# A first transformer layer's out-projection as three rounded fp32r products instead of one fp32 product

## The chip, the cores and the metric

The kernel runs on one core of a Trainium2 chip. The metric is the device time of one execution in microseconds (us). A core has TensorE (PE; its weight loads are listed as PEld), VectorE (DVE), ScalarE (ACT), GpSimd (POOL) and a queue for DMAs on SyncE (SP). Each engine works through its own list of instructions in order and waits on semaphores for the others.

## What is computed

Two transformer layers over 64 x 188 tokens of width 256. Only the first one's attention and FFN touch the change:

```python
h = tok_ref(x, ...)                                  # strided conv, layer norm
h = h + attn_ref(layernorm(h), qkv_proj, qkv_bias, out_proj, out_bias)
h = h + ffn_ref(layernorm(h), w_gate, w_up, w_down)  # fp4-quantized
# in attn_ref: 16 heads of 16, softmax, then
out = einsum('lni,ei->lne', out, out_proj) + out_bias
```

The second layer (linear attention with a cumulative sum, and an FFN) is computed by another function, `layer1`, which the change leaves alone.

## The kernel before

`layer0` handles 94 tiles (`TILES`) of 128 tokens. Its work is a software pipeline: in slot t the conv of tile t, the attention of tile t-1, the out-projection of tile t-2, the FFN's gate and up products of tile t-3 and its down product of tile t-4 are done. `slots` writes out slots 0 to 5 and the last ones and loops over the rest, two slots a turn. Every engine has its own `slot` function, whose order of calls is the order of that engine's instructions; nothing else schedules them. Semaphores in the table `S` tie the engines together: `wait` puts a wait ahead of the next instruction, and what stands behind it on the engine waits too.

TensorE's order in a slot (L469 to L506) is: conv, v_product, xq_transpose, scores, gate(t, 0), att_transpose, hq_transpose, up(t, 0), outproj, gate(t, 1), up(t, 1), down, ln1_transpose, p_transpose, qk_product, pv_product. gate and up compute the FFN in two halves of 352 columns into the psum tensor `gu`. DVE's order (from L874) is: conv_read, xq_low, score_max and score_shift, glu_gate(0), glu_up(0), hq_low, ln0_statistics, h1_add, glu_gate(1), glu_up(1), hq_scales, xq_amax, h2_add and the rest of the rounding of xq, att_divide, hq_round.

Some products are already split: `product3` (L1091 to L1095) computes high x low + low x high + high x high in three fp32r matmuls, where the high part is the value rounded to fp32r and the low part what is left. The conv, gate, up and down products are done so; ACT makes the high part of an activation (xq_copy, hq_copy), DVE the low part by a subtraction (xq_low, hq_low), and TensorE waits for the low part's semaphore.

The out-projection is not split. att_transpose (L398) turns the attention's output `att` into the psum bank `tp`, att_copy on ACT (L597) copies it to `attT`, and outproj (L412) multiplies it in fp32 with `outw_sb`:

```python
wait(pe, "attT_copied", t - 1)
for c in range(KC):
    last = pe.matmul(cv[:, 0:DM], attT[:, c, :], outw_sb[:, c, :], start=c == 0, stop=c == KC - 1)
```

Each fp32 matmul leaves two records in the trace. h1_add on DVE (L810) adds the residual to the result. glu_up (L797) waits for `up_done` of TensorE. The first slots also prepare the weights (weight_scales, weight_round, weight_low on DVE, weight_magnitude and weight_high on ACT).

Of the kernel before, what the change touches and what calls it, by code (L numbers as in the profile page):

```python
# [6 lines left out]
fp32 = mybir.dt.float32  # L7
fp32r = mybir.dt.float32r
# [148 lines left out]
def layer0(nc, x, conv_w, conv_b, tok_g, tok_b, qkv_w, q_b, k_b, v_b, out_w, out_b, gate_w, up_w, down_w,  # L157
           h2_dram, ident, eps, exponent, w1, w1_loaded, wq, wk, wv, wo):
    with ExitStack() as ctx:
        def sb(name, shape, dt=fp32):  # L160
            return ctx.enter_context(nc.sbuf_tensor(name, shape, dt))

        def sem(name):
# [29 lines left out]
        attT = sb("attT", [128, KC, 128])  # L193
# [25 lines left out]
        wconv_hi, wconv_lo = sem("wconv_hi"), sem("wconv_lo")  # L219
        wpad, wtrans, whigh, wlow, wdown = sem("wpad"), sem("wtrans"), sem("whigh"), sem("wlow"), sem("wdown")  # L220
# [13 lines left out]
            "att_transposed", "attT_copied", "outproj_done", "h1_step", "h1b_ready", "ln2_ready", "xq_step", "xabs_ready", "xq_ready",  # L234
# [44 lines left out]
        with nc.Block() as block:  # L279
# [47 lines left out]
            def _(pe):  # L327
# [25 lines left out]
                def xq_transpose(t):  # L353
                    bank_free(pe, t, [("ln1T_copied", t - 1, 1, 1)],
                              [("attT_copied", t - 3, 1, 1), ("xqT_split", t - 4, 1, 1)])
                    wait(pe, "xq_ready", t - 2)
                    transposes(tp, [(128 * c, xq[:, 128 * c:128 * (c + 1)]) for c in range(KC)], "xq_transposed")
# [38 lines left out]
                def att_transpose(t):  # L396
                    bank_free(pe, t, [("xqT_split", t - 3, 1, 1)],
                              [("ln1T_copied", t - 1, 1, 1), ("attT_copied", t - 3, 1, 1)])  # L398
                    wait(pe, "att_step", t - 1, ATT)
                    av = att[:].rearrange("p h d -> p (h d)")  # L400
                    transposes(tp, [(128 * c, av[:, 128 * c:128 * (c + 1)]) for c in range(KC)], "att_transposed")
# [10 lines left out]
                def outproj(t):  # L412
                    bank_free(pe, t, [("y_step", t, YS, 1)], [("h2_ready", t - 5, 1, 1), ("h1_step", t - 3, H1S, 1)])
                    wait(pe, "attT_copied", t - 1)
                    for c in range(KC):
                        last = pe.matmul(cv[:, 0:DM], attT[:, c, :], outw_sb[:, c, :], start=c == 0, stop=c == KC - 1)
                    last.then_inc(S["outproj_done"], 1)
# [9 lines left out]
                def ln1_transpose(t):  # L427
                    bank_free(pe, t, [("attT_copied", t - 2, 1, 1)],
                              [("xqT_split", t - 3, 1, 1), ("ln1T_copied", t - 1, 1, 1)])
                    wait(pe, "ln1_ready", t + 1)  # L430
                    transposes(tp, [(128 * c, ln1[:, 128 * c:128 * (c + 1)]) for c in range(KC)], "ln1_transposed")
# [121 lines left out]
            def _(act):  # L553
# [43 lines left out]
                def att_copy(t):  # L597
                    wait(act, "att_transposed", t - 1)
                    wait(act, "outproj_done", t - 2)
                    copy(attT[:], tp[:, 0:256], "attT_copied")  # L600
# [62 lines left out]
                def slot(t, par):  # L663
# [41 lines left out]
                    if isinstance(t, int) and t == 0:  # L705
                        weight_magnitude("up")
# [42 lines left out]
            def _(dve):  # L749
# [109 lines left out]

                def hq_low(t):  # L860
# [13 lines left out]
                def slot(t, par):  # L874
# [14 lines left out]
                    if exists(t, 3):  # L889
                        glu_gate(t - 3, 0)  # L890
                        glu_up(t - 3, 0)
                    if exists(t, 4):
                        hq_low(t)
# [12 lines left out]
                    if isinstance(t, int) and t == 1:  # L906
                        dve.wait_ge(S["rs1"], 4 * 2)
                        weight_round("up")
                        weight_scales("down", 1)
# [937 lines left out]
```

## Time and profile before

| | us |
|---|---|
| runs of the kernel (3) | 4570.43, 4573.46, 4578.34 |
| median | 4573.46 |
| the profiled execution | 4570.04 |
| its span | 4568.1 |
| TensorE busy | 4362.2 (95%) |
| DVE busy | 3314.3 (73%) |
| ACT busy | 2707.9 (59%) |
| POOL busy | 2089.1 (46%) |

The first layer runs from the start to about 1630 us, the second from there to the end. The profile's rows tell of one execution. A row of the timeline gives start, duration, engine, line of the source, operation and operands; what stands in brackets is the idle time of the engine ahead of the row and who ended it. The ends of matmuls are modelled and overlap with the next one, so the distance between starts is the better measure.

### The profile page before, as it was taken

What the parts mean: (1) busy time and instruction counts of PE and PEld (TensorE: products, weight loads), DVE (VectorE), ACT (ScalarE), POOL (GpSimd) and SP (SyncE); (2) the same over time, 40 slices, a digit from 0 to 9 for tenths busy, and PEclk for the clock granted to TensorE, in tenths of its full rate; (3) what the DMA queues carried; (4) which work ended last, traced back from release to release, by engine and by line L of the source; (5) the groups of instructions that cost most, each with busy time, mean ns of one, the idle gap of its engine ahead of it and who ended that gap; (6) DMA issues with size and microseconds to landing.
All of it is one profiled execution on the core that took longest, in us unless ns stands there. A gap on an engine that the chain in (4) does not pass through costs nothing.

```text
span 4568.1 us, 121671 instructions
## 1 busy us (share of the span) xinstructions
PE 4362.2 (95%) x43948; PEld 3976.4 (87%) x43948; DVE 3314.3 (73%) x7106; ACT 2707.9 (59%) x5662; POOL 2089.1 (46%) x2682
## 2 busy tenths in 40 slices
PE   5999999999999948999999999999999999999997
PEld 5899999999999837899999999999999999989986
DVE  6899999999999844666666666666666666666665
ACT  4777777777777724555555555555555555545553
POOL 4566666666666512443343343343344334334333
PEclk8999999999999969999999999999999999999998
DMA  1100000000000010000000000000000000000000
GB/s 52 61 24 24 24 24 22 24 24 24 24 24 24 21 45 5 5 15 8 9 12 12 8 9 15 9 9 15 8 9 15 9 9 12 12 9 8 15 5 11
DMA packets 64982, 79.21 MB, mean 17 GB/s; under 512 B 8800, under 2 KB 51168, under 8 KB 64480
## 3 DMA queue, kind: packets, MB, share of 16 engines
q1 hardware_dynamic: 64608, 74.07, 5.6%
q8 instruction: 254, 4.16, 0.4%
q14 instruction: 120, 0.98, 0.1%
HBM read 49.40 MB, written 24.64 MB: 16 GB/s over the span
## 4 chain that ended last, share of the span: by engine, by line
PE 57%; DVE 2%; issue 1%; ACT 1%; POOL 1%; DMA 0%; ACTq 0%; DVEq 0%; SPq 0%; POOLq 0%
PE bA L1093 11%; PE bA L1094 10%; PE bA L1095 10%; PE bS L1378 4%; PE bO L1400 3%; PE bA L1462 3%; PE bB L1093 2%; PE bB L1363 2%; PE bB L1364 2%; PE bB L1094 2%; PE bB L1095 2%; PE bA L1463 2%; PE bT L1416 2%; PE bO L1404 1%; PE bO L1409 1%
## 5 line engine op out<-in xcount | busy, mean ns | idle before, releaser
L1793 POOL TENSOR_TENSOR sqs_lo<-sq,sqs_hi 128x768 fp32r<-128x768 f32 x256 | 479.7, 1874 | 677.2 <-ACT sqs_hi L1513 673.4
L1604 DVE TENSOR_TENSOR qk_lo<-bA,qk_hi 128x384 fp32r<-128x384 f32 x512 | 284.3, 555 | 533.1 <-ACT qk_hi L1513 533.0
L1532 ACT ACTIVATE phi<-bB 128x768 f32<-128x768 f32 x256 | 207.3, 810 | 663.0 <-PE bB L1364 663.0
L1751 POOL TENSOR_TENSOR yT_lo<-tanh_y,yT_hi 128x384 fp32r<-128x384 f32 x256 | 259.2, 1013 | 548.4 <-ACT yT_hi L1513 548.4
L1513 ACT ACTIVATE qk_hi<-bA 128x384 fp32r<-128x384 f32 x512 | 251.2, 491 | 202.9 <-PE bA L1095 202.8
L1614 DVE TENSOR_TENSOR aT<-bS,mask 128x1024 f32<-128x1024 f32 x256 | 311.0, 1215 | 1.3 <-PE bS L1383 1.3
L1522 ACT ACTIVATE sq<-bA 128x384 f32<-128x384 f32 x512 | 250.3, 489 | 61.8 <-DVE qk_lo L1604 61.8
L571 ACT ACTIVATE kblk<-gu,kb_masked,rowmask 128x128 f32<-128x128 f32 x752 | 271.0, 464 | 4.6 <-PE gu L452 4.6
L1093 PE MATMUL bA<-fc_lo,yT_hi 128*128 128x256 f32 x768 | 231.2, 301 | 12.8 <-ACT pre L1562 6.1
L1093 PE MATMUL bA<-wv_lo,xT_hi 128*128 128x256 f32 x768 | 229.7, 299 | 5.6 <-ACT sq L1522 1.0
L1093 PE MATMUL bA<-wo_lo,attT_hi 128*128 128x256 f32 x768 | 226.6, 295 | 7.9 <-ACT pre L1562 0.5
L1462 PE MATMUL bA<-hT_lo,fc_w 128*128 128x384 f32 x512 | 213.5, 417 | 19.0 <-DVE xT_lo L1604 12.1
L640 ACT ACTIVATE ln<-h,nbias,rstd 128x256 f32<-128x256 f32 x188 | 113.0, 601 | 189.9 <-POOL nbias L1011 189.9
L1378 PE MATMUL bS<-phi 64*64 64x192 f32 x4096 | 225.5, 335 | 0.0
L1742 POOL TENSOR_TENSOR rstd<-moments,eps 128x3 f32<-128x3 f32 x96 | 18.9, 196 | 451.5 <-DVE moments L1688 451.5
L1400 PE MATMUL bO<-V,aT 128*64 128x65 f32 x4096 | 219.4, 228 | 0.0
L1095 PE MATMUL bA<-fc_hi,yT_hi 128*128 128x256 f32 x768 | 218.2, 284 | 0.0
L1094 PE MATMUL bA<-fc_hi,yT_lo 128*128 128x256 f32 x768 | 218.1, 284 | 0.0
L1094 PE MATMUL bA<-wv_hi,xT_lo 128*128 128x256 f32 x768 | 216.5, 282 | 0.0
L1095 PE MATMUL bA<-wv_hi,xT_hi 128*128 128x256 f32 x768 | 216.4, 282 | 0.0
L1513 ACT ACTIVATE sqs_hi<-sq 128x768 fp32r<-128x768 f32 x256 | 214.6, 838 | 1.5 <-issue 0.3
L1094 PE MATMUL bA<-wo_hi,attT_lo 128*128 128x256 f32 x768 | 213.7, 278 | 0.0
(269 smaller groups left out, 16237.8 us busy)
## 6 DMA issues: line engine op xcount, KB each, us to landing
xT<-in_x SPq DMA_DIRECT2D x94, 256.0 KB, 2.6
h_scratch<-h SPq DMA_DIRECT2D x188, 64.0 KB, 1.9
hx<-h_scratch SPq DMA_DIRECT2D x32, 256.0 KB, 2.7
out<-res SPq DMA_DIRECT2D x32, 256.0 KB, 2.1
hx<-h_scratch SPq DMA_DIRECT2D x64, 64.0 KB, 2.5
out<-res SPq DMA_DIRECT2D x64, 60.0 KB, 1.8
q<-in_fc_q SPq DMA_DIRECT2D x2, 1024.0 KB, 6.3
wq_sb<-in_wq SPq DMA_DIRECT2D x1, 1024.0 KB, 7.0
```

The lines of the kernel that those rows point to most:

```text
L571: act.activation(kblk[:, c, :, j, :], src, ACT.Identity, bias=kb_masked[:, c, j:j + 1], scale=rowmask[:, j:j + 1]).then_inc(S["qk_copied"], 1)
L1093: pe.matmul(out, lhs[0], rhs[1], start=start, stop=False)
L1094: pe.matmul(out, lhs[1], rhs[0], start=False, stop=False)
L1095: return pe.matmul(out, lhs[0], rhs[0], start=False, stop=stop)
L1378: pe.matmul(SC[o:o + 64, h, q], phi[b][p, 1, k], phi[b][p, 0, q], start=True, stop=True)
L1400: pe.matmul(O[o:o + 64, dst(i)], aT[b][:, h, HEADS[i] + o:HEADS[i] + o + 64], V[:, i, v], start=True, stop=True)
L1462: pe.matmul(A[:, k, 0:NT], w, hT[1][:, k, :], start=True, stop=False)
L1513: act.activation(dst, src, ACT.Copy).then_inc(S[done], 1)
L1604: dve.tensor_tensor(dst, src, hi.bitcast(fp32), ALU.subtract).then_inc(S[done], 1)
L1614: dve.tensor_tensor(aT[b][:], SC[:, :, 0:ST], mask[:].unsqueeze(1).broadcast_to([128, 2, ST]), ALU.mult)\
L1751: pool.tensor_tensor(yT[1][:, f % RING, :], tanh_y[f % 2][:], yT[0][:, f % RING, :].bitcast(fp32), ALU.subtract).then_inc(S["y_lo"], 1)
L1793: pool.tensor_tensor(sqs[1][:], sq[:], sqs[0][:].bitcast(fp32), ALU.subtract).then_inc(S["sq_lo"], 1)
```

## The change

`attT` and the weight `outw` become pairs of fp32r tensors, high and low. The out-projection becomes `product3`: six matmuls in place of two. ACT's att_copy writes the high part. A new function att_low on DVE subtracts it from the psum bank and signals `attT_split`; outproj waits for that instead of `attT_copied`, and so do the transposes that reuse the bank `tp`. att_low stands in DVE's slot behind glu_up(t - 3, 0) and ahead of hq_low. The weight is split once: its high part on ACT in slot 0, its low part on DVE in slot 1; outproj of slot 2 waits for it.

```diff
--- before.py
+++ after.py
@@ -190,7 +190,8 @@
         PT = sb("PT_sb", [128, PAIRS, 128])
         rden = sb("rden", [128, H0])
         att = sb("att", [128, H0, D0])
-        attT = sb("attT", [128, KC, 128])
+        attT = sb("attT_hi", [128, KC, 128], fp32r), sb("attT_lo", [128, KC, 128], fp32r)
+        outw = sb("outw_hi", [128, KC, DM], fp32r), sb("outw_lo", [128, KC, DM], fp32r)
         h1 = [sb(f"h1_{i}", [128, DM]) for i in range(2)]
         h1b = [sb(f"h1b{i}", [128, DM]) for i in range(2)]
         ln2 = sb("ln2", [128, DM])
@@ -217,6 +218,7 @@
         wconv, wsmall, wqkv, wout = sem("wconv"), sem("wsmall"), sem("wqkv"), sem("wout")
         wconst, vones, wfold, vbias = sem("wconst"), sem("vones"), sem("wfold"), sem("vbias")
         wconv_hi, wconv_lo = sem("wconv_hi"), sem("wconv_lo")
+        wout_hi, wout_lo = sem("wout_hi"), sem("wout_lo")
         wpad, wtrans, whigh, wlow, wdown = sem("wpad"), sem("wtrans"), sem("whigh"), sem("wlow"), sem("wdown")
         W = {n: {k: sem(f"{n}_{k}") for k in ("loaded", "scales", "scaled", "abs", "round", "ready")}
              for n in ("gate", "up", "down")}
@@ -231,7 +233,7 @@
             "stats_seen", "scores_seen", "rs0", "rs1", "rs2", "x_loaded0", "x_loaded1", "x_high", "x_low", "conv_done", "y_step", "ln0", "gb_step", "st1",
             "ln1_ready", "ln1_transposed", "ln1T_copied", "qk_done", "v_done", "qk_copied", "vblk_ready",
             "scores_done", "shift_step", "probs_ready", "p_transposed", "PT_copied", "pv_done", "att_step",
-            "att_transposed", "attT_copied", "outproj_done", "h1_step", "h1b_ready", "ln2_ready", "xq_step", "xabs_ready", "xq_ready",
+            "att_transposed", "attT_copied", "attT_split", "outproj_done", "h1_step", "h1b_ready", "ln2_ready", "xq_step", "xabs_ready", "xq_ready",
             "xq_transposed", "xqT_copied", "xqT_split", "gate_done", "up_done", "tanh_done", "hh_step", "hqa_step", "hv_ready", "habs_ready", "hqb_step",
             "hq_ready", "hq_transposed", "hqT_copied", "hqT_split", "down_done", "h2_ready", "h2_stored0", "h2_stored1")}
 
@@ -352,7 +354,7 @@
 
                 def xq_transpose(t):
                     bank_free(pe, t, [("ln1T_copied", t - 1, 1, 1)],
-                              [("attT_copied", t - 3, 1, 1), ("xqT_split", t - 4, 1, 1)])
+                              [("attT_split", t - 3, 1, 1), ("xqT_split", t - 4, 1, 1)])
                     wait(pe, "xq_ready", t - 2)
                     transposes(tp, [(128 * c, xq[:, 128 * c:128 * (c + 1)]) for c in range(KC)], "xq_transposed")
 
@@ -395,7 +397,7 @@
 
                 def att_transpose(t):
                     bank_free(pe, t, [("xqT_split", t - 3, 1, 1)],
-                              [("ln1T_copied", t - 1, 1, 1), ("attT_copied", t - 3, 1, 1)])
+                              [("ln1T_copied", t - 1, 1, 1), ("attT_split", t - 3, 1, 1)])
                     wait(pe, "att_step", t - 1, ATT)
                     av = att[:].rearrange("p h d -> p (h d)")
                     transposes(tp, [(128 * c, av[:, 128 * c:128 * (c + 1)]) for c in range(KC)], "att_transposed")
@@ -411,9 +413,12 @@
 
                 def outproj(t):
                     bank_free(pe, t, [("y_step", t, YS, 1)], [("h2_ready", t - 5, 1, 1), ("h1_step", t - 3, H1S, 1)])
-                    wait(pe, "attT_copied", t - 1)
+                    if isinstance(t, int) and t == 2:
+                        pe.wait_ge(wout_lo, 1)
+                    wait(pe, "attT_split", t - 1)
                     for c in range(KC):
-                        last = pe.matmul(cv[:, 0:DM], attT[:, c, :], outw_sb[:, c, :], start=c == 0, stop=c == KC - 1)
+                        last = product3(pe, cv[:, 0:DM], [x[:, c, :] for x in attT], [x[:, c, :] for x in outw],
+                                        c == 0, c == KC - 1)
                     last.then_inc(S["outproj_done"], 1)
 
                 def down(t):
@@ -425,7 +430,7 @@
                     last.then_inc(S["down_done"], 1)
 
                 def ln1_transpose(t):
-                    bank_free(pe, t, [("attT_copied", t - 2, 1, 1)],
+                    bank_free(pe, t, [("attT_split", t - 2, 1, 1)],
                               [("xqT_split", t - 3, 1, 1), ("ln1T_copied", t - 1, 1, 1)])
                     wait(pe, "ln1_ready", t + 1)
                     transposes(tp, [(128 * c, ln1[:, 128 * c:128 * (c + 1)]) for c in range(KC)], "ln1_transposed")
@@ -597,7 +602,7 @@
                 def att_copy(t):
                     wait(act, "att_transposed", t - 1)
                     wait(act, "outproj_done", t - 2)
-                    copy(attT[:], tp[:, 0:256], "attT_copied")
+                    copy(attT[0][:], tp[:, 0:256].rearrange("p (c t) -> p c t", c=KC), "attT_copied")
 
                 def exponentials(t):
                     wait(act, "shift_step", t, SHIFT)
@@ -703,6 +708,8 @@
                         k_copy(t)
                         q_copy(t)
                     if isinstance(t, int) and t == 0:
+                        act.wait_ge(wout, 32)
+                        act.activation(outw[0][:], outw_sb[:], ACT.Copy).then_inc(wout_hi, 1)
                         weight_magnitude("up")
                     if isinstance(t, int) and t == 2:
                         weight_magnitude("down")
@@ -856,6 +863,11 @@
                     wait(dve, "xqT_copied", t - 2)
                     dve.tensor_tensor(xqT[1][:], tp[:, 0:256].rearrange("p (c t) -> p c t", c=KC), xqT[0][:].bitcast(fp32),
                                       ALU.subtract).then_inc(S["xqT_split"], 1)
+
+                def att_low(t):
+                    wait(dve, "attT_copied", t - 1)
+                    dve.tensor_tensor(attT[1][:], tp[:, 0:256].rearrange("p (c t) -> p c t", c=KC), attT[0][:].bitcast(fp32),
+                                      ALU.subtract).then_inc(S["attT_split"], 1)
 
                 def hq_low(t):
                     wait(dve, "hqT_copied", t - 3, 2)
@@ -889,6 +901,8 @@
                     if exists(t, 3):
                         glu_gate(t - 3, 0)
                         glu_up(t - 3, 0)
+                    if exists(t, 2):
+                        att_low(t)
                     if exists(t, 4):
                         hq_low(t)
                     if exists(t, 0):
@@ -904,6 +918,8 @@
                         weight_scales("up", 2)
                         weight_round("gate")
                     if isinstance(t, int) and t == 1:
+                        dve.wait_ge(wout_hi, 1)
+                        dve.tensor_tensor(outw[1][:], outw_sb[:], outw[0][:].bitcast(fp32), ALU.subtract).then_inc(wout_lo, 1)
                         dve.wait_ge(S["rs1"], 4 * 2)
                         weight_round("up")
                         weight_scales("down", 1)
```

TensorE, slot 4, around the out-projection (`gu<-up_...` is the first half's up product, `gu<-gate_...` the second half's gate product). Before:

```order
L1094 MATMUL gu<-up_hi,xqT_lo 128x352
L1095 MATMUL gu<-up_hi,xqT_hi 128x352
L416 MATMUL bank<-outw_sb,attT 128x256 [waits attT_copied,h1_step,y_step]
L416 MATMUL bank<-outw_sb,attT 128x256
L1093 MATMUL gu<-gate_lo,xqT_hi 128x352 [waits hh_step]
L1094 MATMUL gu<-gate_hi,xqT_lo 128x352
```

and after:

```order
L1110 MATMUL gu<-up_hi,xqT_lo 128x352
L1111 MATMUL gu<-up_hi,xqT_hi 128x352
L1109 MATMUL bank<-outw_lo,attT_hi 128x256 [waits attT_split,h1_step,y_step]
L1110 MATMUL bank<-outw_hi,attT_lo 128x256
L1111 MATMUL bank<-outw_hi,attT_hi 128x256
L1109 MATMUL bank<-outw_lo,attT_hi 128x256
L1110 MATMUL bank<-outw_hi,attT_lo 128x256
L1111 MATMUL bank<-outw_hi,attT_hi 128x256
L1109 MATMUL gu<-gate_lo,xqT_hi 128x352 [waits hh_step]
```

The place is the same; the two matmuls are now six, and the first of them waits for attT_split instead of attT_copied.

DVE in the same slot (`hh` is the FFN's hidden value, `bank` the psum bank tp or cv). Before:

```order
L779 TENSOR_REDUCE rowmax<-sc 128x16 [waits scores_done]
L785 TENSOR_TENSOR P<-sc,rowmax 128x1024 [waits shift_step,p_transposed]
L794 SCALAR_TENSOR_TENSOR hh<-tanh_g,gu 128x352 [waits hqb_step,tanh_done]
L801 TENSOR_TENSOR hh<-hh,gu 128x352 [waits hh_step,up_done]
L862 TENSOR_TENSOR hqT_lo<-pt,hqT_hi 128x640 [waits hqT_copied]
L865 TENSOR_TENSOR hqT_lo<-pt,hqT_hi 64x128
L871 BN_STATS stats<-h 128x6 [waits gb_step]
```

and after:

```order
L786 TENSOR_REDUCE rowmax<-sc 128x16 [waits scores_done]
L792 TENSOR_TENSOR P<-sc,rowmax 128x1024 [waits shift_step,p_transposed]
L801 SCALAR_TENSOR_TENSOR hh<-tanh_g,gu 128x352 [waits hqb_step,tanh_done]
L808 TENSOR_TENSOR hh<-hh,gu 128x352 [waits hh_step,up_done]
L869 TENSOR_TENSOR attT_lo<-bank,attT_hi 128x256 [waits attT_copied]
L874 TENSOR_TENSOR hqT_lo<-pt,hqT_hi 128x640 [waits hqT_copied]
L877 TENSOR_TENSOR hqT_lo<-pt,hqT_hi 64x128
```

One instruction is new, attT_lo, directly behind the one that waits for TensorE's up_done.

## Rows read from the trace of the kernel before

**Rows 1.** The page: TensorE's busy time, and the granted clock in 40 slices.

```profile
PE 4362.2 (95%) x43948; PEld 3976.4 (87%) x43948; DVE 3314.3 (73%) x7106; ACT 2707.9 (59%) x5662; POOL 2089.1 (46%) x2682
PEclk8999999999999969999999999999999999999998
```

**Rows 2.** Busy time by stretch: first layer, 600 to 900 us, columns as headed.

```profile
core 0: us, PE busy (x) PEld busy (x) DVE busy (x) ACT busy (x) POOL busy (x), PEclk, DMA share, GB/s
600.00:900.00 300.00, 298.92 (x2913) 270.84 (x2914) 274.03 (x604) 231.31 (x552) 180.73 (x344) 1.00 0.09 25
```

**Rows 3.** Timeline, all engines, one slot around the out-projection.

```profile
805.07 0.38 ACT L555 ACTIVATE attT<-bank 128x256 f32<-128x256 f32 x1
...
806.11 0.32 PE L1095 MATMUL gu<-up_hi,xqT_hi 128*128 128x352 f32 x1
...
806.27 1.02 PE L416 MATMUL bank<-outw_sb,attT 128*128 128x256 f32 x4
806.56 0.52 DVE L801 TENSOR_TENSOR hh<-hh,gu 128x352 f32<-128x352 f32 x1 [0.23 <-PE gu L1095]
...
806.94 0.51 PE L1093 MATMUL gu<-gate_lo,xqT_hi 128*128 128x352 f32 x1
...
807.00 0.82 DVE L862 TENSOR_TENSOR hqT_lo<-pt,hqT_hi 128x640 fp32r<-128x640 f32 x1
...
807.29 0.32 PE L1094 MATMUL gu<-gate_hi,xqT_lo 128*128 128x352 f32 x1
```

**Rows 4.** Timeline, DVE: glu_up(0) in two neighbouring slots.

```profile
166.87 0.52 DVE L801 TENSOR_TENSOR hh<-hh,gu 128x352 f32<-128x352 f32 x1
...
183.26 0.52 DVE L801 TENSOR_TENSOR hh<-hh,gu 128x352 f32<-128x352 f32 x1 [0.16 <-PE gu L1095]
```

**Rows 5.** Timeline, TensorE: two neighbouring fp32r products of the conv.

```profile
800.09 0.28 PE L1094 MATMUL bank<-conv_hi,xT_lo 128*128 128x256 f32 x1
...
800.21 0.28 PE L1095 MATMUL bank<-conv_hi,xT_hi 128*128 128x256 f32 x1
```

**Rows 6.** Timeline: xq's low part on DVE, and the first gate products behind it.

```profile
802.82 0.42 DVE L857 TENSOR_TENSOR xqT_lo<-bank,xqT_hi 128x256 fp32r<-128x256 f32 x1
...
803.39 0.40 PE L1093 MATMUL gu<-gate_lo,xqT_hi 128*128 128x352 f32 x1
...
803.63 0.32 PE L1094 MATMUL gu<-gate_hi,xqT_lo 128*128 128x352 f32 x1
```

**Rows 7.** Waits of weight loads, 300 to 1500 us: us in total, times, longest.

```profile
PEld gu L1093 <- issue: 29.0, 73, 0.5
PEld sc L369 <- issue: 19.6, 73, 0.3
PEld bank L331 <- issue: 12.5, 73, 0.2
```

**Rows 8.** Timelines of the first slots: ACT, DVE and TensorE, by time.

```profile
35.58 1.48 ACT L712 ACTIVATE up_mag<-uraw 128x1536 f32<-128x1536 f32 x1 [1.67 <-POOL uraw L121]
...
46.49 1.76 DVE L127 SCALAR_TENSOR_TENSOR uraw<-up_mag,uraw 128x1536 f32<-128x1536 f32 x1 [1.60 <-POOL nbias L1011]
...
60.11 1.95 PE L416 MATMUL bank<-outw_sb,attT 128*128 128x256 f32 x4 [0.57 <-ACT attT L555]
...
61.43 1.23 DVE L785 TENSOR_TENSOR P<-sc,rowmax 128x1024 f32<-128x1024 f32 x1
...
89.58 0.41 PE L331 MATMUL bank<-ident,ln 128*128 128x128 f32 x2 [2.01 <-ACT ln L640]
```

**Rows 9.** Timeline, TensorE: waits in the last slots of the first layer.

```profile
1595.93 1.09 PE L369 MATMUL sc<-kblk,qT 64*64 64x256 f32 x16 [1.28 <-ACT qT L562]
...
1612.33 0.63 PE L1093 MATMUL gu<-gate_lo,xqT_hi 128*128 128x352 f32 x1 [1.35 <-DVE xqT_lo L857]
```

**Rows 10.** Busy time by stretch, columns as in rows 2.

```profile
90.00:105.00 15.00, 13.30 (x127) 11.22 (x126) 10.48 (x25) 11.36 (x31) 5.12 (x8) 0.89 0.00 1
...
1570.00:1600.00 30.00, 28.22 (x290) 25.37 (x289) 26.44 (x56) 22.37 (x56) 14.71 (x29) 1.00 0.04 11
```

## The prediction

> **What bounds the kernel now.** I read the page first: TensorE (PE) is busy for 95% of the span and its granted clock stands at 9 tenths or more in nearly every slice; the dip near the middle is the change from the first layer to the second [rows 1]. The change lies in the first layer, so the second view is the table by stretches. Between 600 and 900 us TensorE is busy for 298.9 of 300 us at a granted clock of 1.00 and VectorE (DVE) for 274.0 [rows 2]. A slot (one tile of 128 tokens, six tiles deep in the pipeline) lasts 16.39 us: the same DVE instruction of two neighbouring slots starts at 166.87 and 183.26 [rows 4]. Busy matmuls overlap, so the busy share proves little; starts tell more. In the timeline of one slot the last product of the first FFN half starts at 806.11, the out-projection 0.16 later, and the next FFN half follows without a hole [rows 3]. TensorE sets the slot, and a hole put into its queue lengthens every slot unless the hole replaces one that is there.
>
> **The product itself.** Before, two fp32 matmuls (four records) stand between the last up product at 806.11 and the second gate product at 807.29, 1.18 us [rows 3]. Two steps of 0.16 in that belong to FFN products, so the out-projection takes 0.86. After, it is six fp32r products of 256 columns. The conv's products of that form follow each other in 0.12 us [rows 5]: 6 x 0.12 = 0.72. Gain 0.14 us a slot, over 94 slots 13 us. This is all the change can bring.
>
> **The new wait.** Before, outproj waits for ACT's copy of attT, which ends at 805.45, 0.8 us before it is needed. After, it waits for att_low on DVE, which stands behind glu_gate(0) and glu_up(0). glu_up(0) needs the up product that TensorE has only just issued: it starts at 806.56, having sat idle for 0.23 us until TensorE delivered [rows 3]. So TensorE finishes the up half, DVE multiplies it into hh, DVE forms attT's low part, and only then may TensorE go on. Nothing else is queued on TensorE ahead of outproj, and its queue runs in program order, so gate(1), up(1) and down wait too. Counted from the start of the last up product: 0.45 until glu_up starts (806.56); 0.44 until DVE takes the next instruction (hq_low at 807.00 today, att_low then) [rows 3]. att_low has the form of xqT_lo, 0.42, and the same hand-over stands in the trace: xqT_lo ends at 803.24, the first gate product starts at 803.39 and the second, since the stream starts afresh, 0.24 later [rows 6]. That is 0.45 + 0.44 + 0.42 + 0.15 + 0.24 = 1.70 to the second of the six products; four more steps of 0.12 to the sixth, one to the first gate product and 0.16 to the second gate product give 1.70 + 0.48 + 0.12 + 0.16 = 2.46 us, against 1.18 now. **Each slot grows by 1.28 us** (1.42 of hole less 0.14 of product). All slots that have both an FFN and an out-projection pay, t = 3 to 95: 93 x 1.28 = 119 us. The bounds of the hole: without the 0.15 and the 0.12 of a fresh start 1.0 a slot, 93 us; with DVE late by one more 0.42 (below) 1.70, 158 us. I take the middle value, since its two ends are rows of the same operation in the same slot.
>
> **What else moves.** att_low itself never waits on ACT: the copy was done 1.5 us before. Behind it on DVE hq_low comes 0.42 later; its reader, down, stands behind twelve FFN products of 0.16 on TensorE, which themselves start 1.28 later, so it is hidden. ln0's statistics and h1_add also move by some 0.4 us, h1_add now close behind outproj; POOL's and ACT's normalizations follow DVE, but ln1_transpose on TensorE moves by the full 1.28 and gets looser. DVE goes from 15.0 to 15.4 busy us in a slot of 17.7: no bound. ACT's rounded copy of attT costs what the plain one does (0.38, and xqT_hi, which rounds, is copied in the same way). The psum bank that the attT transposes fill is held until att_low has read it; its next writer on TensorE stands behind outproj anyway. DMAs are not touched.
>
> **The weights' split, once.** ACT's outw copy stands before up_mag, where ACT sat idle for 1.67 us; DVE's low part stands before an instruction that waited 1.60 us [rows 8]. For 128x512 elements I take 0.7 on DVE, between 0.42 for 128x256 [rows 6] and 1.76 for 128x1536 [rows 8]. Both are hidden; uncovered they would cost 1.3 us in all.
>
> **Edges.** In slot 2 (no FFN yet) outproj now follows score_max and score_shift: it starts at 60.11, and DVE is busy with the shift from 61.43 for 1.2 us [rows 8]. It comes some 3 us later; what follows waited for DVE's weight work already, so 2 of it count (0 to 3). In slot 3 TensorE waits 2.01 us for ACT's ln later on [rows 8] and swallows about 1.0. The last two slots have no conv, and TensorE has holes of its own (1.35 until xqT_lo) [rows 9]: 1 us swallowed. Together nothing.
>
> **The sum** against the profiled execution's own time: 4570.0 (span 4568.1 and 1.9 around it) + 119 = 4689. The median of the runs shown is 3.4 above that execution, so a median should land between 4689 and 4692: **4690 us**.
>
> **Rivals.**
> *DVE becomes the loop (7%).* Today the DVE chain rowmax, shift, glu_gate arrives at glu_up almost together with TensorE's up product, with 0.23 us to spare [rows 3]. If the additional 0.42 makes DVE the later one at each round, the slot grows by 1.28 + 0.42 = 1.70, +158: 4728 to 4731. Against it: that chain starts anew in each slot from TensorE's scores, and TensorE falls back by more than DVE.
> *Part of the hole is given back (6%).* TensorE's weight loads waited 29.0 + 19.6 + 12.5 us in 73 slots, 0.84 a slot [rows 7]. If all of that went because DVE and ACT come out earlier relative to TensorE, 0.44 a slot stay: 4611. Against it: the largest, before the gate, is a round trip that TensorE itself starts (xq's transposes, ACT's copy, xqT_lo, gate) and no slack elsewhere shortens it; the one before the scores lies inside that round trip.
> *TensorE has room, and the kernel gets faster (4%).* Place: TensorE's queue from outproj to the end of the slot. Weight loads fill 270.8 of 300 us [rows 2], so by that measure 1.6 us of a slot are free, more than the 1.42 of hole, and only the 0.14 saved would count: 4570 - 13 = 4557. It decides once TensorE's free time in a slot passes 1.42 us. The starts speak against it: up, outproj, gate follow each other at their own pitch [rows 3]. The Trainium skill, "Perfetto Trace Analysis", section "Identifying the Most-Contended Engine", says that matmul busy share is not a good measure of distance to the roofline and that the busy share of weight loads is; by that rule there would be the 10% room, while the pitch in this trace shows it is not room that a wait can use.
> *The clock falls (5%).* A new hole of 1.4 us in every slot could bring the granted clock down. Rows: between 90 and 105 us, with holes, 0.89 was granted; between 1570 and 1600 us, with a single wait of 1.28 us at 1595.93, 1.00 [rows 9, 10]. At 0.89 a slot of 16.39 would take 2.0 us more, with the hole 3.3, 93 x 3.3 = +305: 4875. The Trainium skill, "TensorE: Matmul & The Clock Gate", section "A second HAM failure mode: psum-queue depth-cycling", says that a TensorE which idles briefly between groups of matmuls loses throughput to a clock that goes down and up; the single wait in [rows 9] does not show it.
>
> **How the numbers follow.** Forecast 78%, at 4690, itself within 4660 to 4718; rivals 7, 6, 4 and 5%. The range takes in the bounds of the hole from 1.0 to 1.70 a slot: 4660 to 4732. What is left out is the two low rivals, the clock, and a few per cent of the forecast's own. A measurement of this kernel can tell about 0.2%, 9 us, from no change. Faster by more: 4%; within: 1%; slower by more: 95%.
>
> **What would show it.** In the profile after: slots 17.67 us apart; the first outproj product some 1.46 us behind the last up product instead of 0.16, released by attT_lo on DVE; att_low directly behind glu_up(0) at 0.42 us; six products 0.12 apart; TensorE busy near 93% in the first layer, its clock still 1.00; the second layer unchanged. The forecast is wrong if the slot stays near 16.4 (then TensorE was not the bound), if glu_up(0) starts later than 0.45 behind the last up product (DVE loop), or if the clock between 300 and 1500 us falls below 1.

## The result and the profile after

The changed kernel takes 4692.0 us (median of 4 runs, 4690.0 to 4697.0), the kernel before 4575.9 beside it (4 runs, 4570.4 to 4585.0). The ratio is 1.0245, its 95% interval 1.0231 to 1.0259: slower by 2.3 to 2.6%. Forecast were 4690 and a range of 4660 to 4732.

The profiled execution of after took 4693.5 us. Its page, the lines that answer to [rows 1]; below it the table by stretches for 600 to 900 us, which answers to [rows 2] (columns: stretch, length, then busy us and instructions of PE, PEld, DVE, ACT, POOL, granted clock, DMA share, GB/s):

```profile
span 4691.5 us, 122143 instructions
PE 4375.5 (93%) x44136; PEld 3971.4 (85%) x44136; DVE 3366.2 (72%) x7201; ACT 2689.0 (57%) x5663; POOL 2090.7 (45%) x2682
PEclk8999999999999997999999999999999999999998
```

```profile
600.00:900.00 300.00, 279.42 (x2723) 249.42 (x2723) 263.70 (x579) 210.65 (x511) 170.16 (x324) 1.00 0.08 22
```

TensorE was busy for 298.9 of these 300 us before and is for 279.4 now. DVE fell too, from 274.0 to 263.7, with one instruction more in each slot: everything runs at a longer beat. The granted clock stays at 1.00.

How long a slot is, one row says for each kernel: all instances of xqT_lo on DVE (one a slot) with the first and last start between 300 and 1500 us. First before, then after:

```profile
L857 DVE TENSOR_TENSOR xqT_lo<-bank,xqT_hi x73: 405/423/425, 310.7 to 1491.8; 128x256 fp32r<-128x256 f32 x73
```

```profile
L864 DVE TENSOR_TENSOR xqT_lo<-bank,xqT_hi x68: 423/424/426, 311.1 to 1492.3; 128x256 fp32r<-128x256 f32 x68
```

Before: 1181.1 us over 72 slots, 16.40. After: 1181.2 over 67, 17.63. Growth 1.23 us a slot. The same row is the measure of every experiment below.

The timeline of after, around the out-projection of one slot; it answers to [rows 3]:

```profile
825.74 0.32 PE L1111 MATMUL gu<-up_hi,xqT_hi 128*128 128x352 f32 x1
826.19 0.52 DVE L808 TENSOR_TENSOR hh<-hh,gu 128x352 f32<-128x352 f32 x1 [0.28 <-PE gu L1111]
826.63 0.42 DVE L869 TENSOR_TENSOR attT_lo<-bank,attT_hi 128x256 fp32r<-128x256 f32 x1
827.19 0.36 PE L1109 MATMUL bank<-outw_lo,attT_hi 128*128 128x256 f32 x1 [1.14 <-DVE attT_lo L869]
827.39 0.28 PE L1110 MATMUL bank<-outw_hi,attT_lo 128*128 128x256 f32 x1
827.98 0.33 PE L1109 MATMUL gu<-gate_lo,xqT_hi 128*128 128x352 f32 x1
828.15 0.33 PE L1110 MATMUL gu<-gate_hi,xqT_lo 128*128 128x352 f32 x1
```

This is the relay that was forecast: last up product 825.74, glu_up 0.45 later, att_low 0.44 later for 0.42, TensorE 0.14 after that. From the last up product to the second gate product it is 2.41 us, against 1.18 before [rows 3]: 1.23 more, the growth of the slot.

The waits of after between 300 and 1500 us (engine, line, what was waited for: us in all, times, longest), the lines that answer to [rows 7] and the new one:

```profile
PE bank L1109 <- DVE attT_lo L869: 76.9, 68, 1.1
PEld gu L1109 <- issue: 34.5, 68, 0.5
DVE hh L808 <- PE gu L1111: 16.4, 68, 0.3
PEld sc L371 <- issue: 11.5, 68, 0.2
```

The new wait stands once in each of 68 slots. DVE waits for TensorE at glu_up in every one (0.24 each), so DVE did not become the loop.

The second layer's first DVE instruction dates the end of the first layer, before and after:

```profile
L1200 DVE MEMSET half<- x1: 165/165/165, 1656.5 to 1656.5; 128x128 f32 x1
```

```profile
L1216 DVE MEMSET half<- x1: 165/165/165, 1771.9 to 1771.9; 128x128 f32 x1
```

The first layer is 115.4 us longer: 93 slots x 1.23 = 114, and 1 for the edges. What follows, unchanged code, took 2911.6 us before and 2919.6 after. In the profiles of the experiments the same stretch took 2909 to 2920 us, so the 8 are its scatter and not the change's.

### The profile page after: what moved, and what is told of

Read it like the earlier page. It is cut to its first block, busy times and chain, and to the rows that moved or that the text cites. A ratio compares the mean times of both kernels' runs of the same rounds, so it can differ in the third digit from the quotient of the medians.

```text
span 4691.5 us, 122143 instructions
## 1 busy us (share of the span) xinstructions
PE 4375.5 (93%) x44136; PEld 3971.4 (85%) x44136; DVE 3366.2 (72%) x7201; ACT 2689.0 (57%) x5663; POOL 2090.7 (45%) x2682
## 4 chain that ended last, share of the span: by engine, by line
PE 56%; DVE 2%; issue 1%; ACT 1%; POOL 1%; DMA 0%; ACTq 0%; DVEq 0%; SPq 0%; POOLq 0%
PE bA L1109 11%; PE bA L1110 9%; PE bA L1111 9%; PE bS L1394 4%; PE bO L1416 3%; PE bA L1478 3%; PE bB L1109 2%; PE bB L1380 2%; PE bB L1379 2%; PE bB L1110 2%; PE bB L1111 2%; PE bA L1479 2%; PE bT L1432 2%; PE bO L1420 1%; PE bO L1425 1%
## 5 line engine op out<-in xcount | busy, mean ns | idle before, releaser
L1111 PE MATMUL bA<-wo_hi,attT_hi 128*128 128x256 f32 x768 | 213.2, 278 | 0.0
```

What stands on the lines that cost most here:

```text
L1111: return pe.matmul(out, lhs[0], rhs[0], start=False, stop=stop)
```

## The experiments

**Theory.** TensorE's in-order queue stands while glu_up(0) and att_low run on DVE; that hand-over is the whole loss, and the product is worth 0.14 us a slot. The hole, below, is the time in which TensorE stands ahead of the out-projection. **Rivals:** the six products themselves cost something; DVE's additional work costs wherever it stands; the slot is set by something else than TensorE. Each run is compared with runs of the kernel before on the same chip (medians 4577.3, 4574.2 and 4577.8 in the three groups).

### Wait or product: each alone

`wait_alone`: the kernel before with its fp32 product; DVE subtracts behind glu_up(0), and outproj waits for that.

```diff
-                    wait(pe, "attT_copied", t - 1)
+                    wait(pe, "attT_split", t - 1)
+                def att_low(t):
+                    wait(dve, "attT_copied", t - 1)
+                    dve.tensor_tensor(attT_lo[:], tp[:, 0:256].rearrange("p (c t) -> p c t", c=KC), attT[:],
+                                      ALU.subtract).then_inc(S["attT_split"], 1)
```

> The kernel before with its fp32 out-projection, to which only DVE's subtraction (into a tensor that nothing reads) is added behind glu_up(0), and outproj waits for it; no part of the computation is left out. Serial hand-over (TensorE's up product, glu_up(0), att_low, TensorE): first out-projection record 1.46 us behind the last up product instead of 0.16, slot 16.39 + 1.37 = 17.76 us, 93 slots, about 4700 us (+2.8%). If the six products or their operands cost the time instead: slot near 16.4, about 4575 us. If the clock fell: granted clock below 1.00 between 300 and 1500 us.

Measured: 4692.7 us, ratio 1.0257 (1.024 to 1.0275). Slot and out-projection:

```profile
L858 DVE TENSOR_TENSOR xqT_lo<-bank,xqT_hi x67: 424/425/426, 313.0 to 1483.8; 128x256 fp32r<-128x256 f32 x67
619.38 1.10 PE L417 MATMUL bank<-outw_sb,attT 128*128 128x256 f32 x4 [1.14 <-DVE attT_lo L863]
```

The slot is 17.74 us, with the same 1.14 us of idle TensorE ahead of the product. The wait makes the loss; the six products save 17.74 - 17.63 = 0.11 us a slot beside it.

`product_alone`: after, without att_low. The low part of attT is left out and the high part stands in its place, so that the six products remain and outproj waits for ACT's copy as before.

```diff
-                    wait(pe, "attT_split", t - 1)
+                    wait(pe, "attT_copied", t - 1)
-                        last = product3(pe, cv[:, 0:DM], [x[:, c, :] for x in attT], [x[:, c, :] for x in outw],
+                        last = product3(pe, cv[:, 0:DM], [attT[0][:, c, :]] * 2, [x[:, c, :] for x in outw],
```

> The changed kernel with six fp32r products but without att_low: outproj waits for ACT's copy only, and the high part of attT stands in for the low part (attT's low part is left out of the result). Serial hand-over: no hole, 0.72 us for six products in place of 0.86, slot 16.25 us, about 4562 us (-0.3%). If the products cost the time: slot near 17.6, about 4690 us.

Measured: 4574.8 us, ratio 0.9997 (0.9988 to 1.0007), slot 16.39. The expectation (16.25, 4562) was missed: there is no gain. Slot and waits of product_alone, and its last up product and second gate product around one out-projection:

```profile
L864 DVE TENSOR_TENSOR xqT_lo<-bank,xqT_hi x73: 404/406/408, 311.3 to 1491.6; 128x256 fp32r<-128x256 f32 x73
```

```profile
PEld sc L371 <- issue: 25.7, 73, 0.4
PE sc L371 <- issue: 2.7, 17, 0.2
PE sc L371 <- ACT qT L567: 0.7, 4, 0.2
```

```profile
822.82 0.32 PE L1104 MATMUL gu<-up_hi,xqT_hi 128*128 128x352 f32 x1
823.85 0.33 PE L1103 MATMUL gu<-gate_hi,xqT_lo 128*128 128x352 f32 x1
```

From the last up product to the second gate product it is 1.03 us here (1.04 over all slots), against 1.18 before [rows 3]; from the first product of up(0) to the first of up(1) it is 2.73 instead of 2.87. The 0.14 is there. It is given back later in the slot, ahead of the scores: the weight loads wait 25.7 us instead of 19.6 [rows 7], and TensorE itself waits 2.7 + 0.7 us, lines that the waits of before don't have. These 9.5 us in 73 slots are 0.13 a slot. Something other than TensorE holds the slot at 16.39.

### Where att_low stands, and what outproj waits for

`early` puts att_low ahead of glu_gate(0), `between` between glu_gate(0) and glu_up(0). The diff is that of early:

```diff
+                    if exists(t, 2):
+                        att_low(t)
                     if exists(t, 3):
                         glu_gate(t - 3, 0)
                         glu_up(t - 3, 0)
-                    if exists(t, 2):
-                        att_low(t)
```

> The changed kernel with att_low ahead of glu_gate(0) on DVE; same instructions on all engines. Serial hand-over: att_low ends about when the last up product starts, so a hole of 0.1 us is left, and DVE, 0.3 us later at h1_add, presses on down by 0.1 to 0.2: slot 16.3 to 16.5 us, 4565 to 4585 us. If the 0.42 us of load on DVE were what lengthens the slot, wherever it stands: slot near 17.6, about 4690 us.

> The changed kernel with att_low between glu_gate(0) and glu_up(0) on DVE. Serial hand-over: att_low starts 0.44 behind glu_gate(0), ends about 0.57 us after the last up product's start, hand-over 0.15: first out-projection product at 0.7 instead of 0.16, slot 16.25 + 0.6 = 16.9 us, about 4615 us (+1.0%). If only the load counts: about 4690 us.

Measured: early 4597.8 us, 1.0047 (1.003 to 1.0064), slot 16.63, some 0.1 above the expected span; between 4615.4 us, 1.0092 (1.0072 to 1.0111), slot 16.85, as expected. The timeline of early, around the out-projection:

```profile
618.27 0.41 DVE L869 TENSOR_TENSOR attT_lo<-bank,attT_hi 128x256 fp32r<-128x256 f32 x1
618.50 0.32 PE L1111 MATMUL gu<-up_hi,xqT_hi 128*128 128x352 f32 x1
618.60 0.51 DVE L801 SCALAR_TENSOR_TENSOR hh<-tanh_g,gu 128x352 f32<-128x352 f32 x1
618.83 0.36 PE L1109 MATMUL bank<-outw_lo,attT_hi 128*128 128x256 f32 x1
```

The same of between:

```profile
607.59 0.32 PE L1112 MATMUL gu<-up_hi,xqT_hi 128*128 128x352 f32 x1
607.75 0.41 DVE L869 TENSOR_TENSOR attT_lo<-bank,attT_hi 128x256 fp32r<-128x256 f32 x1
608.31 0.35 PE L1110 MATMUL bank<-outw_lo,attT_hi 128*128 128x256 f32 x1 [0.40 <-DVE attT_lo L869]
```

From the last up product to the first outproj product it is 0.33 in these rows of early, 0.72 in between, 1.45 in after. Four fifths of the loss go with two calls exchanged (after lost 4692 - 4577 = 115 us, early loses 21): the work on DVE is the same, only what it stands behind is not. But early is still 21 us above before.

`twice` does att_low's subtraction two times, the first into a spare tensor.

```diff
                     wait(dve, "attT_copied", t - 1)
+                    dve.tensor_tensor(attT_spare[:], tp[:, 0:256].rearrange("p (c t) -> p c t", c=KC), attT[0][:].bitcast(fp32),
+                                      ALU.subtract)
                     dve.tensor_tensor(attT[1][:], tp[:, 0:256].rearrange("p (c t) -> p c t", c=KC), attT[0][:].bitcast(fp32),
                                       ALU.subtract).then_inc(S["attT_split"], 1)
```

> The changed kernel with one more subtraction of the same form ahead of att_low, into a tensor that nothing reads; nothing is left out. Serial hand-over: the additional instruction lies on the way from TensorE's up product to outproj, so it is paid in full at the distance between two such instructions, 0.34 to 0.44 us: slot 17.63 + 0.4 = 18.0 us, about 4727 us. If DVE's place in the chain did not matter: slot 17.63, about 4692 us.

Measured: 4716.5 us (2 runs), 1.0305 (1.0271 to 1.034), slot 17.95, where 4727 and 18.0 were expected. Its timeline:

```profile
607.21 0.42 DVE L870 TENSOR_TENSOR attT_spare<-bank,attT_hi 128x256 fp32r<-128x256 f32 x1
607.55 0.41 DVE L872 TENSOR_TENSOR attT_lo<-bank,attT_hi 128x256 fp32r<-128x256 f32 x1
608.11 0.35 PE L1112 MATMUL bank<-outw_lo,attT_hi 128*128 128x256 f32 x1 [1.46 <-DVE attT_lo L872]
```

The second subtraction starts 0.34 behind the first, TensorE's idle time grows from 1.14 to 1.46, the slot by 0.32. DVE's time behind glu_up(0) goes one to one into the slot, at the distance between the two starts (0.34) and not at the printed duration (0.42).

`low_last` puts the four products that don't need the low part first, and waits for it only ahead of the last two.

```diff
+                    wait(pe, "attT_copied", t - 1)
+                    for c in range(KC):
+                        pe.matmul(cv[:, 0:DM], attT[0][:, c, :], outw[1][:, c, :], start=c == 0, stop=False)
+                        pe.matmul(cv[:, 0:DM], attT[0][:, c, :], outw[0][:, c, :], start=False, stop=False)
                     wait(pe, "attT_split", t - 1)
                     for c in range(KC):
-                        last = product3(pe, cv[:, 0:DM], [x[:, c, :] for x in attT], [x[:, c, :] for x in outw],
-                                        c == 0, c == KC - 1)
+                        last = pe.matmul(cv[:, 0:DM], attT[1][:, c, :], outw[0][:, c, :], start=False, stop=c == KC - 1)
```

> The changed kernel, with outproj's four products that need only attT's high part first, behind the copy's semaphore, and the two with the low part behind attT_split; att_low stays behind glu_up(0). Serial hand-over: the four products (0.47 us) move into the hole, the hand-over itself stays: slot 17.63 - 0.47 = 17.16 us, about 4648 us. If the wait were not the cause: 17.63.

Measured: 4633.6 us (2 runs), 1.0124 (1.0094 to 1.0154), slot 17.07, where 4648 and 17.16 were expected. The last up product, and the first row of low_last's last two products:

```profile
612.62 0.32 PE L1114 MATMUL gu<-up_hi,xqT_hi 128*128 128x352 f32 x1
613.98 0.50 PE L424 MATMUL bank<-outw_hi,attT_lo 128*128 128x256 f32 x2 [0.56 <-DVE attT_lo L872]
```

The idle time shrinks from 1.14 to 0.56, the slot by 0.56. The four products that fill the hole are 0.47 of it; the first product behind the wait also starts 1.36 behind the last up product instead of 1.45.

`out_behind_gate` moves outproj behind gate(t, 1), so that six products of 0.16 stand between up(0) and it (in slot 2 it stays).

```diff
-                    if exists(t, 2):
+                    if isinstance(t, int) and t == 2:
                         outproj(t)
                     if exists(t, 3):
                         gate(t, 1)
+                    if exists(t, 2) and not (isinstance(t, int) and t == 2):
+                        outproj(t)
+                    if exists(t, 3):
                         up(t, 1)
```

> The changed kernel with outproj behind gate(t, 1) on TensorE in all slots but slot 2; DVE's order as changed. Serial hand-over: six gate products (0.96 us) cover most of the 1.3 us hole, 0.4 stays: slot 16.25 + 0.4 = 16.65 us on TensorE. A second ring, which the runs so far point to (rowmax to xq's scaling on DVE, then ACT's magnitude, k_copy, q_copy, TensorE's scores, rowmax), has 16.39 + 0.34 - 0.09 = 16.64 us with att_low in it. Both give 4596 to 4605 us. If a later out-projection holds up h1_add and with it down: above 16.8.

Measured: 4615.4 us, 1.0084 (1.0056 to 1.0113), slot 16.81, 0.15 longer than expected. TensorE no longer waits for att_low, but the waits have a new line:

```profile
PEld gu L1112 <- DVE hh L804: 25.2, 72, 0.4
```

gate(t, 1) needs glu_gate(0) to have read its psum half. Before and after, the out-projection stands between and no such wait is listed; without it 0.35 us a slot come to light. They are not what sets this slot: the table at the end of the next section shows that a ring through DVE does.

### What holds the slot at 16.4, and at 16.63

A ring is a chain of hand-overs through several engines that comes back to where it began one slot later; its length is then a lower bound of the slot. Two candidates: the rest of a hole on TensorE in early (0.33 where 0.16 stood before), or a ring through DVE, in which att_low's 0.33 counts. `early_low_last` has both edits: the hole ahead of the out-projection is closed (1.04 us from the last up product to the second gate product, as in product_alone), and DVE has the same work as in early.

> att_low ahead of glu_gate(0), and the products with the low part last. On TensorE no hole is left, 16.25 us a slot. If TensorE sets the slot: 16.25 to 16.39 us, about 4565 us. If the ring over DVE and ACT sets it, which holds att_low's 0.34 us wherever it stands between rowmax and xq's scaling: still 16.63 us as with att_low early alone, about 4597 us.

Measured: 4595.0 us, 1.0048 (1.0032 to 1.0064), slot 16.64. Slots of early and of early_low_last, and the latter's waits:

```profile
L864 DVE TENSOR_TENSOR xqT_lo<-bank,xqT_hi x72: 404/407/408, 315.8 to 1496.7; 128x256 fp32r<-128x256 f32 x72
```

```profile
L867 DVE TENSOR_TENSOR xqT_lo<-bank,xqT_hi x73: 405/407/408, 299.9 to 1497.8; 128x256 fp32r<-128x256 f32 x73
```

```profile
PE sc L371 <- ACT qT L570: 11.9, 55, 0.3
```

The slot did not move, and TensorE now waits for ACT's qT in 55 slots. So what sets this slot is not TensorE's own queue. A ring through DVE fits: before, DVE stood at glu_up for TensorE now and then, and att_low's 0.33 (618.27 to 618.60 above) swallows that first. The row of before, and its wait for ACT's binade_x, which the next group aims at:

```profile
DVE hh L801 <- PE gu L1095: 6.9, 37, 0.2
DVE ln L127 <- ACT binade_x L558: 35.2, 73, 0.5
```

6.9 us in 73 slots are 0.09; 16.39 + 0.33 - 0.09 = 16.63. In out_behind_gate att_low stands behind glu_up, whose wait for TensorE stays (6.0 us in 72 slots), so the 0.09 is not to be taken off there.

The next group tried to shorten this ring. DVE has a hole of 0.48 us in it (35.2 in 73), when it waits for ACT's binade_x. The edit moves h2_add(t - 4), 0.41 us, from ahead of the rounding of xq into that hole, in four kernels: before, product_alone (with the same part left out), early and early_low_last. The diff of before_h2:

```diff
-                    if exists(t, 4):
-                        h2_add(t - 4, par)
...
+                    if exists(t, 4):
+                        h2_add(t - 4, par)
```

The first place is behind hq_scales and xq_amax and ahead of xq's inverse scales; the second is between xq_scaled and xq_round.

> The kernel before with h2_add alone moved behind xq's scaling; nothing left out. If TensorE and the ring over DVE and ACT are equally long today (16.39 us), the shorter ring brings nothing: 16.37 to 16.40 us, no difference in time. If the ring alone set the slot: 16.1 to 16.3 us, up to 25 us faster.

> product_alone (six products, no att_low; attT's low part left out) with h2_add on DVE moved behind xq's scaling, into the 0.48 us in which DVE waits for ACT's magnitude. Ring over DVE and ACT (rowmax to xq's scaling, ACT's magnitude, k_copy, q_copy, scores): it shrinks by 0.33 us, TensorE becomes the bound and its 0.14 us comes out: slot 16.25 us, about 4561 us (-0.3%), against 16.39 in product_alone. If the gain of the product was not there because of TensorE itself (six products no cheaper than two fp32 ones): 16.39.

> att_low ahead of glu_gate(0), h2_add moved behind xq's scaling; nothing left out. The ring is 16.63 - 0.33 = 16.30 us; TensorE keeps a hole of 0.21 us ahead of outproj, 16.25 + 0.27 = 16.5 us. Slot 16.5 us, about 4585 us. If the ring were not what set 16.63: still 16.63, 4597 us.

> As early_h2, and the products with attT's low part last; nothing left out. Both rings short: DVE and ACT 16.30, TensorE 16.25 to 16.3 us. Slot 16.3 us, about 4567 us: 0.2% faster than the kernel before. If the ring theory is wrong: 16.63 as without the move, 4595 us.

Measured: before_h2 0.9999 (0.999 to 1.0008), slot 16.40; product_alone_h2 1.0004 (0.9995 to 1.0013), 16.39; early_h2 1.0058 (1.0043 to 1.0074), 16.63; early_low_last_h2 1.0053 (1.0039 to 1.0066), 16.63. No slot moved; only the first was as expected (16.25, 16.5 and 16.3 stood for the others). The hole is gone, though: the line of binade_x is missing in the waits of before_h2. The timelines of before and of before_h2 show why that is worth nothing:

```profile
812.37 1.39 POOL L121 TENSOR_TENSOR hh<-hh,small 128x704 f32<-128x704 f32 x1 [1.14 <-DVE small L109]
812.49 0.41 DVE L822 TENSOR_TENSOR h<-bank,h1b 128x256 f32<-128x256 f32 x1
812.82 0.97 DVE L105 TENSOR_SCALAR small_x<-small_x 128x16 f32<-128x16 f32 x1
813.82 0.17 DVE L107 TENSOR_SCALAR small_x<-small_x 128x16 f32<-128x16 f32 x1
```

```profile
814.90 1.39 POOL L121 TENSOR_TENSOR hh<-hh,small 128x704 f32<-128x704 f32 x1 [1.07 <-DVE small L109]
815.13 1.19 DVE L105 TENSOR_SCALAR small_x<-small_x 128x16 f32<-128x16 f32 x1
```

L105 on 128x16 elements ends at 813.79 in the one and 816.32 in the other, each 0.03 behind the end of POOL's multiplication (813.76 and 816.29). So it is in every slot between 300 and 1500 us of the traces of all fourteen kernels (0.027 to 0.034). With h2_add gone from ahead of it, it starts earlier and lasts longer by the same amount. DVE does not wait in the sense of the view of waits; it is counted busy. The ring runs through POOL's 1.39 us, and h2_add was in its shadow already.

The traces allow the ring to be measured in parts, as means over all slots between 300 and 1500 us:

| us | rowmax to POOL's L121 | L121 to next rowmax | qT's end to scores | rest of TensorE's slot |
|---|---|---|---|---|
| before | 8.89 | 7.52 | 0.24 | 15.22 |
| product_alone | 8.88 | 7.52 | 0.24 | 15.35 |
| early | 9.12 | 7.52 | 0.24 | 15.31 |
| early_low_last | 9.12 | 7.52 | 0.24 | 15.60 |
| out_behind_gate | 9.28 | 7.53 | 0.24 | |
| between | 9.01 | 7.84 | 0.51 | 15.20 |
| low_last | 9.33 | 7.74 | 0.45 | 15.20 |
| after | 9.70 | 7.93 | 0.50 | 15.23 |
| wait_alone | 9.85 | 7.89 | 0.51 | 15.18 |
| twice | 10.03 | 7.92 | 0.50 | 15.22 |

The first two columns add up to the slot. The first goes from rowmax over the shift, both glu pairs and hq_scales on DVE to the start of POOL's multiplication of hh; the second from there over L105 and xq's scaling on DVE, binade_x, k_copy and q_copy on ACT and the scores on TensorE to the next rowmax. The third says whether TensorE takes up the scores as soon as ACT has written qT. The last is what TensorE needs outside the stretch around the out-projection: from the second gate product to the last up product of the next slot.

In the upper five kernels the scores start 0.24 us behind qT in each single slot (0.236 to 0.241), and the second part is the same to 0.01: TensorE takes them up as soon as qT allows, every time, and the ring sets the slot. att_low adds 0.23 to the first part in early and early_low_last (0.33 less the 0.09 that glu_up no longer waits) and 0.39 in out_behind_gate (0.33, and 0.06 by which h1_add starts later still). In the lower five the ring has room, and what TensorE needs outside the out-projection is 15.2 us: its own queue sets the slot. The kernel before shows both signs, 0.24 and 15.22. Its two loops are equally long, to some 0.02 us. No run shortened the ring; forming xq's inverse scales on DVE before POOL's multiplication begins would be the edit to try, and it was not tried.

## Why the prediction was right, and where not

**The relay** was right in each term: 0.45 to glu_up (forecast 0.45), 0.44 to att_low (0.44), 0.42 for it (0.42), 0.14 to TensorE (0.15), 0.20 for the fresh start (0.24), 0.76 to the second gate product (0.76). 2.41 instead of 2.46; the slot grew by 1.23 instead of 1.28, the first layer by 115 instead of 119 us. Outside this stretch TensorE's slot did not change (15.22 and 15.23 in the table above). wait_alone shows the cause by itself, twice and low_last its size from both sides.

**The edges** were right in sum and not in their parts. The first out-projection product of slot 2 starts at 63.77, against 60.11 [rows 8], 3.7 late where "some 3" stood, of which 2 were to count. Of that and of the holes at both ends 1.6 us were swallowed between the out-projections of slots 3 and 6 (the lag behind the kernel before grows from 4.94 to 7.07 us, three slots of 1.23 would give 3.7) and 1.3 between slots 89 and 95 (108.79 to 114.91); 1.0 stood for each. The remainder over the whole layer is 1 us, where nothing was forecast.

**"TensorE sets the slot"** was half of the truth, and one step built on it failed. The reading behind it, products at their own pitch and hardly an idle moment on TensorE, was right, and TensorE's own way through a slot is as long as the slot: the 15.22 us outside the out-projection are what it needs in after too, where the hole does set the slot. What the reading could not show is the ring through DVE, POOL and ACT of the same 16.39 us. "Gain 0.14 us a slot ... This is all the change can bring" was thus wrong where it stood alone: product_alone gained nothing measurable, although TensorE by itself would have needed only 15.22 + 1.04 = 16.26 (an estimate from the table). The forecast did not suffer by it, since the hole makes TensorE's way the longer of the two by more than a microsecond, and beside a hole the product does count: 0.11 between wait_alone and after. That the term came out right in the sum is in part luck: had the hole been small, as in early, the ring would have swallowed it and added 0.24 of its own.

**"What else moves".** That DVE would be no bound at 15.4 us busy in a slot of 17.7 held for after, but not as a rule: with the hole out of the way (early) att_low costs 0.24 a slot, though DVE is busy for 15.3 of 16.63 us (1103.1 of 1200 between 300 and 1500).

**The rivals.** DVE as the loop: refuted, glu_up still waits for TensorE, in all 68 slots now. A part given back: the wait of the weight loads ahead of the scores gave back 0.10 a slot (0.27 before, 11.5 in 68 now), but the one ahead of the gate took 0.51 instead of 0.40 (34.5 in 68, 29.0 in 73), and nothing is left. TensorE with room: the share of weight loads fell from 90 to 83% with a slot 7% longer; the rule quoted from the Trainium skill, "Perfetto Trace Analysis", section "Identifying the Most-Contended Engine", would have promised room that no wait could use in this trace. The clock: it stayed at 1.00 with an idle time of 1.14 us in TensorE every 17.6 us. The Trainium skill, "TensorE: Matmul & The Clock Gate", section "A second HAM failure mode: psum-queue depth-cycling", describes a clock that goes up and down when TensorE idles between groups; holes of this size and spacing did not bring it about.

## What to carry to other kernels

When a cheap instruction is put on another engine's in-order queue, price it by what it stands behind: here 0.42 us of subtraction cost 1.23 a slot behind an instruction that TensorE itself had to feed, and 0.24 two calls earlier. Ask of a saving on the busiest engine whether a ring of round trips through the others is as long. Products that follow each other without a hole do not answer that. The distance from another engine's result to the instruction that needs it does: if it is the same smallest value in every slot (0.24 us from qT to the scores here), the engine waits there each time, however short the wait. An instruction many times longer than its equals of the same shape can be a wait that the profile counts as work.

## What was unexpected in the hardware

A DVE instruction can be held up by POOL though no semaphore ties it to it. L105 is a tensor_scalar from SBUF to SBUF. Its two forms before, and the small one in before_h2 (min/median/max ns):

```profile
L105 DVE TENSOR_SCALAR small<-small x73: 185/185/188, 303.0 to 1484.0; 128x44 f32<-128x44 f32 x73
L105 DVE TENSOR_SCALAR small_x<-small_x x73: 972/976/981, 304.3 to 1485.4; 128x16 f32<-128x16 f32 x73
```

```profile
L105 DVE TENSOR_SCALAR small_x<-small_x x73: 1180/1184/1187, 306.6 to 1487.6; 128x16 f32<-128x16 f32 x73
```

The larger form, with POOL's multiplication not running, takes 0.185 us; L107, of the smaller form and begun behind the end of that multiplication, takes 0.17. L105 of the smaller form, begun behind its start, takes 0.976 and 1.184, to its end in both timelines. h2_add, which reads one operand from psum, takes its usual 0.41 in the middle of the same POOL instruction. The Trainium skill, "SBUF — State Buffer", section "SBUF: two separate sides", has the rule: DVE and GpSimd share a pair of ports, held by whichever instruction starts first for all of its duration, while the other blocks, if the DVE instruction is of a form that uses the pair. The trace agrees, at 0.79 and 1.00 us of standing (0.976 and 1.184 less 0.185); that this form uses the pair is concluded from the two kernels and not seen by itself.
